# Local attention of a decoder: probabilities turned by TensorE instead of scores made twice

## The reference, cut to what matters

```python
qkv = x @ Wqkv                     # x is [4, 512, 128], tokens of half the width shifted by one
q, k = l2norm(q) * qs, l2norm(k) * ksc
q = q * cos * scale + rotate_half(q) * sin * scale
k = k * cos / scale + rotate_half(k) * sin / scale
# each window of 32 queries sees its own 32 keys and the 32 before
sim = jnp.einsum('bhwie,bhwje->bhwij', bq, bk2) * 8.0
sim = jnp.where((it < jb) | (it > jb + 32) | (jb == -1), -big, sim)
attn = jax.nn.softmax(sim, -1)
out = jnp.einsum('bhwij,bhwje->bhwie', attn, bv2)      # then out @ Wo, and the feed-forward part with a gelu
```

## Time and profile before

| | us |
|---|---|
| median of 3 runs | 5161.87 (5161.16 to 5163.03) |
| the profiled execution | 5163.37 |
| its span | 5161.6 |
| TensorE busy | 4068.8 (79%) |
| VectorE busy | 3241.6 (63%) |
| ScalarE busy | 2677.9 (52%) |
| GpSimd busy | 1247.6 (24%) |

### The profile page before, as it was taken

The page is one execution under the profiler, slowest core; times in us unless marked ns, Lnnn a source line. Parts: engine busy times, 40 slices in busy tenths (PEclk is TensorE's granted clock), DMA queues, the critical chain, the costliest instruction groups (busy, mean ns, idle before and its releaser), DMA issues. The chain is left out here.

```text
span 5161.6 us, 126690 instructions
## 1 busy us (share of the span) xinstructions
PE 4068.8 (79%) x45549; PEld 2390.4 (46%) x45678; DVE 3241.6 (63%) x5957; ACT 2677.9 (52%) x5510; POOL 1247.6 (24%) x2886
## 2 busy tenths in 40 slices
PE   2004767876768889596997578999999999999997
PEld 1003333432332222243443336777777777777775
DVE  7996434554437677444555327777777777777775
ACT  2024723554546767361224445666666666666664
POOL 0010200111201111110000144444444444444443
PEclk7556977997879989796998679999999999999998
DMA  2000020000010000001442001000000000000000
GB/s 57 0 0 1 2 69 23 2 1 1 1 33 1 1 2 1 11 2 49 140 135 61 5 9 42 6 10 25 6 28 6 6 28 6 10 24 6 28 6 11
DMA packets 60834, 110.23 MB, mean 21 GB/s; under 512 B 11399, under 2 KB 43251, under 8 KB 59164
## 3 DMA queue, kind: packets, MB, share of 16 engines
q1 hardware_dynamic: 59558, 101.70, 6.7%
q0 software_dynamic: 784, 1.80, 0.2%
HBM read 96.06 MB, written 1.74 MB: 19 GB/s over the span
## 5 line engine op out<-in xcount | busy, mean ns | idle before, releaser
L676 DVE TENSOR_REDUCE minus_max<-banks 128x1 f32<-128x512 f32 (+4 forms) x1152 | 606.1, 570 | 321.6 <-PE banks L571 315.2
L641 ACT ACTIVATE probs<-banks 128x512 f32<-128x512 f32 (+4 forms) x1152 | 581.0, 556 | 339.1 <-PE banks L609 336.8
L2961 POOL TENSOR_TENSOR loc_cos_part<-loc_cos_part,loc_sin_part 128x512 f32<-128x512 f32 x388 | 495.0, 1276 | 658.3 <-DVE loc_sin_part L3390 657.8
L3034 PE MATMUL banks<-loc_w_qkv,loc_shifted 128*128 128x256 f32 x1552 | 389.2, 394 | 15.1 <-DMA loc_adder_of<-loc_head_ones 15.1
L609 PE MATMUL banks<-q_stack,k_stack 64*128 64x512 bf16 (+3 forms) x1152 | 254.5, 381 | 98.9 <-DMA q_stack<-max_rows 71.4
L3423 DVE TENSOR_TENSOR loc_headsT<-banks,loc_sum_inv 128x512 f32<-128x512 f32 x192 | 132.7, 691 | 279.0 <-ACT loc_sum_inv L3295 279.0
L3034 PEld LDWEIGHTS banks<-loc_w_qkv,loc_shifted 128*128 128x128 f32 x1552 | 282.2, 192 | 53.8 <-DMA loc_w_qkv<-in_L_ffn_Wqkv_dram 15.5
L622 PE MATMUL banks<-probs,pair_rows 128*32 128x512 f32 (+3 forms) x2304 | 296.1, 590 | 0.0
L3415 DVE TENSOR_REDUCE loc_minus_max<-banks 128x4 f32<-128x384 f32 x386 | 197.1, 552 | 151.1 <-PE banks L3101 150.4
L700 POOL CAST max_parts<-minus_max 128x8 bf16<-128x8 f32 x192 | 36.7, 191 | 1038.0 <-DVE minus_max L676 1038.0
L1987 PE MATMUL banks<-identity,srt_b 128*128 128x128 f32 x64 | 11.2, 320 | 344.5 <-DVE srt_b L2267 344.5
(11 more groups left out here) (524 smaller groups left out, 9405.0 us busy)
## 6 DMA issues: line engine op xcount, KB each, us to landing
expert_share<-limited_rows SPq DMA_DIRECT2D x136, 256.0 KB, 3.9
expert_w<-in_L_ffn_pairs_dram SPq DMA_DIRECT2D x84, 192.0 KB, 2.3
loc_w_qkv<-in_L_ffn_Wqkv_dram SPq DMA_DIRECT2D x7, 1536.0 KB, 7.8
expert_share<-grouped_rows SPq DMA_DIRECT2D x32, 256.0 KB, 3.9
q_stack<-max_rows SPq DMA_DIRECT2D x384, 3.0 KB
loc_v_edge<-loc_v SPq DMA_DIRECT2D x192, 32.0 KB, 1.8
fixed_w<-in_L_ffn_experts_dram SPq DMA_DIRECT2D x8, 514.5 KB, 3.6
loc_pack<-in_L_ffn_pack_dram SPq DMA_DIRECT2D x6, 537.5 KB, 4.1
```

The costliest lines, as they stand in the source:

```text
L641: nc.scalar.activation(probs[(a % 2) * C + k][e][0:kn, q0:S], t_bank[e][0:kn, q0:S], ACT.Exp, scale=scale).then_inc(s["exp_done"], 1)
L676: nc.vector.tensor_reduce(minus_max[:, u, e, qs[0]:qs[0] + len(qs)], view, AX.X, ALU.max, negate=True).then_inc(s["max_done"], 1)
L2961: nc.gpsimd.tensor_tensor(cos_part[:, tiles, :], cos_part[:, tiles, :], sin_part[:, tiles, :], ALU.add).then_inc(s["summed"], 1)
L3034: ins = nc.tensor.matmul(g.bank[3 * j][:, (t % 2) * QK:(t % 2 + 1) * QK], xs[:, t * P:(t + 1) * P], w_qkv[:, ds(at, QK)], start=True, stop ...
```

## The change: what it does

The scores are made once, with queries on the partitions. ScalarE takes their exp there, with minus the maximum as bias, and gets the sums over the keys from the same instruction (`exps`, now 8 instructions of 128 columns, L3243). GpSimd raises the sums to the power -1 and multiplies the probabilities by the result (`divide_probs`). TensorE turns the normalised probabilities, 8 transposes a step (`turn_probs`), ScalarE copies them out of PSUM (`copy_probs`), and `values` multiplies them by v as before, without the sums. `turn_max`, `split_max`, `turned`, `copy_rows`, `inverse_sums` and their tiles go. 1/norm is computed by a power on GpSimd (`inverse_norms`) in place of a logarithm and an exp on ScalarE. The direct scores stand in banks 0 and 2 instead of 2 and 3, 128 columns for each tile of queries instead of 96, with 32 masked ones in front; so `qk(n + 2)` now waits for the exps of step n's first head, in place of the maxima. q and k have one buffer each instead of two. Four small DMAs that filled `loc_adder_of` at the start go.

```diff
@@ -2961,28 +2948,25 @@
...
-                def floor_norms(m, j):
+                def inverse_norms(m, j):
...
+                    pool.wait_ge(s["norms_done"], m * 2 + (j + 1))
                     nc.gpsimd.tensor_scalar(floored[:, part], norm_sq[:, part], 1e-24, None,
                                             ALU.max).then_inc(s["floored_done"], 1)
-
-                def split_max(m):
...
-                    nc.gpsimd.tensor_copy(pieces[0], minus_max[:, :, :]).then_inc(s["first_done"], 1)
...
+                    pool.wait_ge(s["floored_done"], m * 2 + (j + 1))
+                    when(pool, "rotated_done", m * 2 + (j - 1))
+                    nc.gpsimd.tensor_tensor(inv_norm[:, part], floored[:, part], g.power[:, part],
+                                            ALU.pow).then_inc(s["inverse_done"], 1)
+
+                def divide_probs(m):
+                    for h in range(2):
+                        pool.wait_ge(s["exp_done"], m * 2 * QT + (h + 1) * QT)
+                        nc.gpsimd.tensor_tensor(inv_sums[:, h, :], sums[:, h, :], minus_one[:, :],
+                                                ALU.pow).then_inc(s["inv_sums_done"], 1)
+                        pool.wait_ge(s["inv_sums_done"], m * 2 + (h + 1))
+                        seen = by_query[:, h].rearrange("p w t r k -> p w (t r) k")
+                        nc.gpsimd.tensor_tensor(seen, seen, inv_sums[:, h, :].unsqueeze(1).unsqueeze(3).to_broadcast(
+                            [P, 2, QT, BLOCK]), ALU.mult).then_inc(s["probs_ready"], 1)
...
@@ -3028,8 +3014,8 @@
...
-                    if j == 1:
-                        when(pe, "max_done", m * 2 - 2)
+                    if j == 0:
+                        when(pe, "exp_done", (m - 2) * 2 * QT + QT)
...
@@ -3042,15 +3028,6 @@
...
-                def turn_max(n):
...
@@ -3062,69 +3039,60 @@
...
-                def turned(n, u):
+                def turn_probs(n):
 
                     when(pe, "heads_done", n)
-                    pe.wait_ge(s["rows_copied"], n + 1)
+                    pe.wait_ge(s["probs_ready"], n * 2 + 2)
                     for h in range(2):
-                        nc.tensor.matmul(g.bank[4 + h][:, 0:SPAN], adder_of[h][:, :], adder[:, :],
...
-                                    ins = nc.tensor.matmul(g.bank[4 + h][r * BLOCK:(r + 1) * BLOCK, cols],
...
-                def direct(m, u):
-
-                    pe.wait_ge(s["squared"], m * 2 + 4)
-                    pe.wait_ge(s["turned_by"], m * 4 + 8)
+                        for t in range(QT // 2):
+                            first = 2 * t * SEEN
+                            before = g.bank[4 + h][:, first:first + 2 * SEEN].rearrange("p (e c) -> p e c", e=2)
+                            own = g.bank[4 + h][:, WINDOW + first:WINDOW + first + 2 * SEEN].rearrange("p (e c) -> p e c", e=2)
+                            ident = g.ident[:, :].rearrange("p (e c) -> p e c", e=2)
+                            nc.tensor.transpose(before[:, :, 0:BLOCK], by_query[:, h, 0, t].rearrange("p r k -> p (r k)"), ident)
+                            ins = nc.tensor.transpose(own[:, :, 0:BLOCK], by_query[:, h, 1, t].rearrange("p r k -> p (r k)"),
+                                                      ident)
+                        ins.then_inc(s["probs_turned"], 1)
...
+                    when(pe, "exp_done", m * 2 * QT)
...
-                        nc.tensor.matmul(g.bank[2 + h][:, 0:SPAN], g.ident_bf[:, :], band_direct[:, :, :],
+                        nc.tensor.matmul(score_banks[h][:, :], g.ident_bf[:, :], band_direct[:, :, :],
...
+                                ins = nc.tensor.matmul(score_banks[h][e * BLOCK:(e + 1) * BLOCK, cols],
+                                                       qT[rows, first:first + BLOCK], kT[rows, first:first + SEEN],
...
-                    hold(pe, s, s["exp_done"], n * 2 + 2)
-                    for first, of_v in ((0, True), (HALF, False)):
...
-                                        if not of_v:
-                                            lhs = ones[keys, :]
...
+                    pe.wait_ge(s["turned_copied"], n * 2 + 2)
+                    for j in (*range(NB), -1):
...
+                                    ins = nc.tensor.matmul(g.bank[4 + r][at, qs], lhs, probs[keys, h, cols],
+                                                           start=(j == 0), stop=False, skip_group_check=True)
...
@@ -3181,14 +3149,6 @@
...
-                        turn_max(n)
...
-                        project_v(n + 1, next_v)
...
@@ -3197,16 +3157,26 @@
...
                         turn_qk(n + 1)
-                        turned(n, u)
-                        direct(n + 1, 1 - u)
+                        turn_probs(n)
+                        if hp == LAST:
+                            pe.wait_ge(s["xv_done"], k + 2)
+                        project_v(n + 1, next_v)
+                        direct(n + 1)
+                        values(n, u)
...
@@ -3255,44 +3221,36 @@
...
-                def inverse_norms(m, j):
...
-                    nc.scalar.activation(norm_log[:, part], floored[:, part], ACT.Ln).then_inc(s["norm_log_done"], 1)
...
-                    nc.scalar.activation(inv_norm[:, part], norm_log[:, part], ACT.Exp,
-                                         scale=-0.5).then_inc(s["inverse_done"], 1)
...
-                def copy_rows(n):
...
-                def exps(n):
...
+                def exps(m):
+                    when(act, "probs_turned", m * 2)
                     for h in range(2):
-                        nc.scalar.activation(probs[:, h, :], g.bank[4 + h][:, 0:SPAN], ACT.Exp).then_inc(s["exp_done"], 1)
-
-                def inverse_sums(n):
...
-                    nc.scalar.activation(sum_log[:, :].rearrange("p (r q) -> p r q", r=2), sum_part,
-                                         ACT.Ln).then_inc(s["sum_log_done"], 1)
...
-                    nc.scalar.activation(sum_inv[:, :], sum_log[:, :], ACT.Exp, scale=-1.0).then_inc(s["sum_inv_done"], 1)
+                        act.wait_ge(s["max_done"], m * 2 + (h + 1))
+                        for t in range(QT):
+                            r, at = t // 2, (t % 2) * 2 + t // 2
+                            nc.scalar.activation(by_query[:, h, :, t % 2, r, :],
+                                                 score_banks[h][:, t * 2 * BLOCK:(t + 1) * 2 * BLOCK].rearrange(
+                                                     "p (w k) -> p w k", w=2), ACT.Exp,
+                                                 bias=minus_max[:, t, h:h + 1],
+                                                 accum_out=sums[:, h, at:at + 1]).then_inc(s["exp_done"], 1)
+
+                def copy_probs(n):
+                    when(act, "values_done", n)
+                    for h in range(2):
+                        act.wait_ge(s["probs_turned"], n * 2 + (h + 1))
+                        nc.scalar.activation(probs[:, h, :], g.bank[4 + h][:, 0:SPAN], ACT.Copy).then_inc(s["turned_copied"], 1)
...
@@ -3325,20 +3283,16 @@
...
-                        if not isinstance(n, int) or n > 0:
-                            inverse_sums(n - 1)
                         square_part(n + 2, 0)
                         square_part(n + 2, 1)
-                        copy_rows(n)
+                        copy_qT(n + 1)
+                        copy_kT(n + 1)
+                        copy_probs(n)
                         copy_v(n + 1, 1 - u)
-                        copy_qT(n + 1, 1 - u)
-                        copy_kT(n + 1, 1 - u)
                         if hp == 5:
                             when(act, "y_done", k)
                             lower_half((k + 1) % B)
-                        exps(n)
-                        inverse_norms(n + 2, 0)
-                        inverse_norms(n + 2, 1)
+                        exps(n + 1)
...
@@ -3410,19 +3360,18 @@
...
-                    when(dve, "third_done", m)
+                    when(dve, "exp_done", m * 2 * QT)
...
-                                                g.bank[2 + h][:, 0:SPAN].rearrange("p (t j) -> p t j", t=QT),
+                                                score_banks[h][:, :].rearrange("p (t j) -> p t j", t=QT)[:, :, WINDOW:2 * BLOCK],
...
-                    dve.wait_ge(s["sum_inv_done"], n + 1)
...
                         dve.wait_ge(s["o_ready"], o_parts)
-                    nc.vector.tensor_tensor(headsT[:, hp * S:(hp + 1) * S].rearrange("p (r q) -> p r q", r=2), value_part,
-                                            sum_inv[:, :].rearrange("p (r q) -> p r q", r=2),
-                                            ALU.mult).then_inc(s["heads_done"], 1)
+                    nc.vector.tensor_copy(headsT[:, hp * S:(hp + 1) * S].rearrange("p (r q) -> p r q", r=2),
+                                          value_part).then_inc(s["heads_done"], 1)
...
```

181 lines of the change are left out of this document (51 added, 130 removed).

## The result

| | before | after |
|---|---|---|
| median | 5162.02 (5161.16 to 5163.03, 4 runs) | 5538.82 (5536.56 to 5549.2, 4 runs) |
| ratio | | 1.0734 [1.0715, 1.0752] |
| span of the profiled execution | 5161.6 | 5546.7 |

The change makes the kernel 7.3% slower: +377 us, where +594 was forecast. The direction and the engine were right; the forecast loss was 1.6 times the measured one.

What follows compares the result with a forecast made beforehand. TensorE bounds the kernel before, GpSimd after: 12.01 + 1.1 port + 0.2 and 0.15 holes = 13.46 us a step, 3.06 over 10.40; x 192 = 588, + 5 at the start = 593, giving 5756 us (8 in 10: 5480 to 6010).

Steps and rivals of the forecast that it cites:

- TensorE's part: TensorE's matmuls in the last stage: removed less added work saves 1.35 us a step, down to 9.05.
- GpSimd's part: GpSimd's list in the last stage: powers, multiplications, additions, floors and waits sum to 12.01 us a step, the deciding term.
- self-waits: GpSimd waiting for its own last result next to each of four powers: 0.18 us each, 0.74 a step.
- The port between GpSimd and VectorE: VectorE's normalisation of q and k, twice a step, pushes GpSimd back: 1.1 us a step, at most 1.28.
- Idle GpSimd: Holes at the gelus of up to 1.7 us, 0.2 a step, and layer norm z instructions delayed, 0.15 a step.
- The ring doesn't set the step: Dependences through several engines take 10.8 us a step, 11.4 with a port wait, below GpSimd's 13.1, so no bound.
- the ring: Chain from GpSimd's powers and multiplications through TensorE's transposes, v, scores, first maximum and four exps to GpSimd: 10.8 us.
- TensorE waits there anyway, so it is hidden: Feed-forward matmuls after the values fall into TensorE's wait for the first exps, so they add no time.
- Rival 3: Faster than before: powers cost 0.25 us like other small operations, GpSimd 7.5 and ring 9.8 a step; 5048 us, chance 0.03.
- Rival 2: The ring takes over at a lower TensorE clock: 14.3 to 15 us a step, 5920 to 6050 us; chance 0.20, shared.
- Rival 1: GpSimd bounds but cheaper, without port waits and holes: 12.01 us a step, 5478 us; chance 0.14.
- The signs looked for: What the new profile would show in the last stage if right, such as GpSimd over 85% busy, or if wrong.

Runs made afterwards that it cites:

- short_powers: The changed kernel with its four GpSimd powers a step replaced by subtractions of the same tiles, so its results are not the reference's: 5132.45 us, ratio 0.9938.
- extra_gpsimd: The changed kernel with one more 128x4 power a step on GpSimd, ahead of the division, into a tile nobody reads: 5640.35 us, ratio 1.0923.
- v_first: The changed kernel with the v projection, and its copy on ScalarE, moved ahead of the probabilities' transposes and their copies: 5465.87 us, ratio 1.0592.
- busy_tensor: The changed kernel with eight unread bf16 matmuls of 512 columns before TensorE's wait for the normalised probabilities: 5468.21 us, ratio 1.0590.
- norms_on_scalar: The changed kernel with 1/norm again from a logarithm and an exp on ScalarE, placed behind the eight exps: 5449.71 us, ratio 1.0556.
- norms_first: The changed kernel with 1/norm from a logarithm and an exp on ScalarE, placed ahead of the eight exps: 5247.41 us, ratio 1.0168.
- short_v_hole: short_powers with the v projection moved, in three of eight steps, ahead of the q and k projections: 5074.79 us, ratio 0.9828.
- before_norm_powers: The kernel before the change with only 1/norm moved to a power on GpSimd: 5403.36 us, ratio 1.0475.

## Why the prediction was right in sign and engine, and off in size

**TensorE's part: right.** 1.35 us a step less was forecast; where the clock is nearly full (short_powers, 0.98) it is 1.38. In the changed kernel itself the busy time is 1299.22 / 137.9 = 9.42; short_powers has the same TensorE instructions and 8.84, so the 0.58 between them goes with the lower clock.

**GpSimd's part: right in kind.** The terms, forecast and measured, us a step:

| term | forecast | measured |
|---|---|---|
| additions | 2.55 | 2 x 1.274 = 2.55 |
| powers 128x8 | 3.34 | 2 x 1.668 = 3.34 |
| powers 128x4 | 2.07 | 2 x 1.048 = 2.10 |
| multiplications | 2.55 | 2 x 1.041 = 2.08 |
| floors, port waits in them | 0.50 + 1.1 | 2 x 0.401 = 0.80 |
| self-waits | 0.74 | about 4 x 0.08 = 0.3 |

The slope from two power rows gave the price of the third size within 3 ns (1671 against 1668), and an exponent of -1 costs what -0.5 does (128x4: 1.01 in the median against 1.04). The mis-sized term is the multiplication: I priced it as the addition of the same size. It takes 1.04. It differs from the addition in its repeated operand and in its operation, and no run tells which of the two makes it shorter. The self-waits were read as 0.18 from one place; between floor and power it is 4207.66 - (4206.89 + 0.69) = 0.08, between a power and its multiplication 4210.38 - (4209.30 + 1.01) = 0.07.

**The port between GpSimd and VectorE: the step that failed most, 1.1 forecast, about 0.3 measured on GpSimd.** The mechanism was right for the additions. At 4206.31 the normalisation meets the addition of 4205.66, lasts 1.17 and ends 0.55 after it; the floor then takes 0.69. It is the earlier trace rows over again. By the Trainium skill (SBUF — State Buffer, "Who interferes with whom") the lock is held for the whole instruction and the other side waits; the trace agrees for the additions, and it does not for the powers, of which I had said that by it they would hold VectorE up. What failed is that I charged every normalisation to GpSimd. From 3300 us on, 108 of 356 normalisations start while an addition runs, and they take 1.67 us in the median. But 183 start while a power runs, as at 4209.42, and they take 0.68 to 0.72, no longer than those that meet nothing (0.69); the 128x8 powers keep their 1.668. The powers fill so much of GpSimd's list that half of the normalisations fall beside them and cost next to nothing. And VectorE pays as well: its normalisation has a mean of 0.901 us in the stretch, 0.4 us a step above the undisturbed two, and VectorE, at 65% busy, had time to spare.

**Idle GpSimd: 0.35 forecast beside the self-waits, about 1.1 measured.** It waits 82.5 us in the stretch for the rotary products, 31.4 before the powers of the sums, nearly all for exps, and 28.2 for sums of squares. The wait for the rotary products is 4.8 us a batch, 3.5 of it in the step of the gelus, where I had allowed a hole of up to 1.7. So the terms above were 1.7 us a step too high (multiplications 0.47, floors and port 0.80, self-waits 0.44), and the idle time 0.7 too low; the forecast came out 1.13 high, 13.46 instead of 12.33. (The measured terms with the instructions that come once a batch, 0.24, add up to 11.1 and not to 10.94, because the records of GpSimd overlap a little.)

**"The ring doesn't set the step": this step failed in its form.** I compared one number for GpSimd's list with one for the ring and took the larger. (The ring with one wait for the port, 11.4, is 1.7 below 13.1, not 1.9.) The batch has steps of eight lengths. The changed kernel's are 13.17, 9.94, 14.03, 10.57, 14.21, 12.80, 12.24 and 11.39 us (`hp` 0 to 7). A list of 10.94 is below six of them and above two, so in some steps GpSimd is late and in others something else is. extra_gpsimd shows it from one side (half of its 1.01 us appears), v_first, busy_tensor and norms_on_scalar from the other. I had also left out of the ring its second branch, by way of 1/norm, normalisation and the turning of q and k; norms_on_scalar against norms_first puts 202 us on it when 1/norm is late.

**"TensorE waits there anyway, so it is hidden": wrong where TensorE has nothing to hide.** The feed-forward work fills that wait in four of eight steps only. short_powers and short_v_hole show that the wait for exps stays when GpSimd is no longer late. Rival 3's figure, 5048, was worked out with the powers at 0.25: the run with 0.27 took 5132. A ring of 9.8 was its bound, and the mean step is 10.22.

**Rival 2 (the lower clock) was partly true.** The ring wasn't wholly at the lower level; the stretch was granted 0.94, which cost about 71 us or more (busy_tensor), inside a time below the forecast. Rival 1 (GpSimd bounds, but cheaper; 5478) is the nearer of the two to what happened: 5539 lies between it and my forecast, because most of the port waits that I had added did not come.

**The signs looked for.** GpSimd over 85% busy: 89%. Gelu loads 107 to 108 us apart: 98.67. Powers 1.67 and 1.04: yes. Multiplication 1.28 to 1.9: 1.04. Exps 0.39 from start to start: 0.34 to 0.36 (4206.03 to 4206.39). GpSimd idle over 2 us a step, which would have spoken for the ring: 1.39, so by that sign alone neither case was clear, and that is how it turned out.

**The account.** From before to after, us: TensorE's work -265 and its waits for exps and the rest +235 (short_powers together -30); the length of the powers +406. Part of the 406 comes by the clock that the waits pull down: busy_tensor won 71 of it back, and TensorE's busy time gives an estimate of the most that the longer matmuls can be, 0.58 x 192 = 111. The split within the 406 was not measured apart. Of the powers, those for 1/norm are 291 when the logarithm and exp are put back in the best place tried.

## What to carry to other kernels

Before a transcendental moves to an idle engine, read its row there: a power of eight elements in each partition took GpSimd longer (1.67 us) than adding two tiles of 512 (1.27), and the logarithm and exp that it replaced took ScalarE 0.42 us together (in the kernel before, same stretch):

```profile
L3261 ACT ACTIVATE loc_norm_log<-loc_floored 128x8 f32<-128x8 f32 x328 | 68.9, 210 | 89.9 <-POOL loc_floored L2969 89.9
L3264 ACT ACTIVATE loc_inv_norm<-loc_norm_log 128x8 f32<-128x8 f32 x328 | 68.6, 209 | 10.5
```

An engine that is 70% busy can still cost 4.7% (before_norm_powers), if long instructions stand ahead of short ones on the path; the order of four 0.2 us instructions was worth 202 us. When one engine's list and the ring are within 2 us of each other, don't take the larger of two means: lay out the kinds of steps and take it in each.

## What the runs showed of the hardware that I had not expected

- A GpSimd multiplication of 128x512 f32 with one operand repeated along 64 columns takes 1.041 us, the addition of two whole tiles 1.274. A power of 4, 6 and 8 columns takes 1.04, 1.35 and 1.67 us.
- The collisions of the two engines depend on what GpSimd runs and who starts first. A power of 128x4 that starts while a normalisation runs is held up: at 4202.39 in norms_on_scalar it took 1.45 us in place of 1.04. A normalisation that starts while a power runs is not: 183 of 183 in the changed kernel took 0.68 to 0.72. A normalisation that starts while an addition runs takes 1.67 in the median, and the floor behind that addition 0.68 in place of 0.24.
- Useless matmuls can make a kernel faster: 1.7 us of them a step in a pause of TensorE raised the granted clock of the stretch from 0.94 to 0.99 and took 71 us off.
